# ScalarE scales the whole last h, POOL adds up unit 14, unit 0's k and v products go by batch, and both ends of the order are new

## The reference

```python
h = layernorm(x)
q, k, v, g = h @ Wq.T, h @ Wk.T, h @ Wv.T, h @ Wg.T     # 8 heads of 16
q, k = rope(q), rope(k)
kv = einsum('bshd,bshe->bhde', k, v); ksum = k.sum(1); vsum = v.sum(1)
num = einsum('bshd,bhde->bshe', q, kv) * scale + vsum
den = einsum('bshd,bhd->bsh', q, ksum) * scale + 256
o = num / den + conv5(v)                                # 5 taps along the rows, and a bias
x = x + (o * g) @ Wo.T
h2 = layernorm(x)
y = fp8_round(h2 / s_in) @ fp8_round(K / s_k) * (s_in * s_k)
x = x + bf16(y) + bias
```

## Time and profile before

| | us |
|---|---|
| median of 3 runs | 168.31 (168.03 to 168.59) |
| the profiled execution | 168.34 |
| its span, from the first instruction to the last | 166.5 |
| PE busy | 151.6 (91%) |
| DVE busy | 149.7 (90%) |
| POOL busy | 133.9 (80%) |
| ACT busy | 125.6 (75%) |

### The profile page before, as it was taken

One profiled execution on the slowest core, in us unless ns is written; L12 is line 12 of the kernel. 1 busy time (PEld: TensorE's weight loads), 2 busy tenths in 40 slices (PEclk: granted clock), 3 DMA queues, 4 the chain that ended last, 5 costly groups with the idle time before them and its releaser, 6 DMA issues.

```text
span 166.5 us, 3671 instructions
## 1 busy us (share of the span) xinstructions
PE 151.6 (91%) x1047; PEld 122.7 (74%) x1047; DVE 149.7 (90%) x279; ACT 125.6 (75%) x342; POOL 133.9 (80%) x162
## 2 busy tenths in 40 slices
PE   7599989999999999999999999999999999998530
PEld 2176888896868888888979786898978788875410
DVE  1368999989989999999999999999999999999583
ACT  4769791666997889788898998856698887666931
POOL 1456898784989799989999989968879797998850
PEclk9999999999999999999999999999999999999985
DMA  4931520210151617252736132227122423104113
GB/s 140 274 122 41 128 63 17 52 32 4 33 126 32 195 32 210 76 138 65 216 127 164 56 100 63 65 45 238 35 77 58 96 76 84 31 4 157 65 63 126
DMA packets 16390, 15.51 MB, mean 93 GB/s; under 512 B 8944, under 2 KB 10352, under 8 KB 16368
## 3 DMA queue, kind: packets, MB, share of 16 engines
q1 hardware_dynamic: 15936, 14.99, 32.9%
q10 hardware_dynamic: 432, 0.26, 0.6%
HBM read 5.02 MB, written 4.19 MB: 55 GB/s over the span
## 4 chain that ended last, share of the span: by engine, by line
PE 56%; DVE 17%; issue 11%; ACT 7%; POOL 6%; DMA 2%; DVEq 1%; ACTq 0%; POOLq 0%
PE bank L1276 6%; PE bank L1302 6%; PE p_num L1321 6%; DVE acc L981 6%; PE p_num L1313 6%; PE bank L1266 6%; PE bank L1340 6%; PE bank L1257 5%; PE bank L1284 5%; PE bank L1249 4%; PE bank L1330 3%; PE bank L1292 3%; ACT h L441 2%; POOL rs L661 2%; DMA xs<-in_x_dram 2%
## 5 line engine op out<-in xcount | busy, mean ns | idle before, releaser
L981 DVE SCALAR_TENSOR_TENSOR acc<-bank,columns,acc 128x510 f32<-128x510 f32 (+1 forms) x48 | 34.7, 723 | 0.3 <-ACT outer L413 0.3
L441 ACT ACTIVATE h<-x,nmr,rs 128x128 bf16<-128x128 f32 x60 | 24.7, 483 | 3.8 <-POOL nmr L664 3.3
L383 ACT ACTIVATE h<-xs,nmr,rs 128x128 f32<-128x128 f32 x64 | 26.2, 484 | 0.5 <-POOL nmr L653 0.5
L661 POOL TENSOR_TENSOR rs<-ve,minus_half 128x4 f32<-128x4 f32 (+1 forms) x17 | 16.6, 977 | 10.0 <-ACT ve L432 10.0
L697 POOL TENSOR_TENSOR k<-k_turned 128x512 f32<-128x512 f32 x16 | 20.4, 1274 | 4.5 <-DVE k_turned L966 4.5
L706 POOL TENSOR_TENSOR acc<-acc,outer 128x508 f32<-128x508 f32 x16 | 20.3, 1267 | 2.3 <-DVE acc L981 2.3
L650 POOL TENSOR_TENSOR rs<-ve,minus_half 128x4 f32<-128x4 f32 (+1 forms) x17 | 16.6, 976 | 5.7 <-ACT ve L374 5.6
L966 DVE TENSOR_TENSOR k_turned<-bank,turn_k 128x1024 f32<-128x1024 f32 x16 | 19.5, 1220 | 1.2 <-PE bank L1266 0.9
L690 POOL TENSOR_TENSOR qT<-q_turned,q_swapped 128x512 f32<-128x512 f32 x16 | 20.4, 1274 | 0.1
L954 DVE TENSOR_TENSOR q_turned<-bank,turn_q 128x1024 f32<-128x1024 f32 x16 | 19.5, 1217 | 0.9 <-PE bank L1257 0.7
L1302 PEld LDWEIGHTS bank<-v,k 128*128 128x128 f32 x128 | 16.6, 190 | 4.5 <-issue 3.1
(11 more groups left out here) (81 smaller groups left out, 334.7 us busy)
## 6 DMA issues: line engine op xcount, KB each, us to landing
q_swapped<-q_turned SPq DMA_DIRECT2D x32, 128.0 KB, 2.3
xs<-in_x_dram SPq DMA_DIRECT2D x15, 256.0 KB, 3.3
out_dram<-ob SPq DMA_DIRECT2D x15, 256.0 KB, 2.5
xs<-in_x_dram SPq DMA_DIRECT2D x2, 128.0 KB, 2.9
turn_q<-in_turn_q_dram SPq DMA_DIRECT2D x1, 256.0 KB, 4.5
out_dram<-ob SPq DMA_DIRECT2D x2, 128.0 KB, 2.0
h2T<-h SPq DMA_TRANSPOSE x14, 2.4
w_qk<-in_w_qk_dram ACTq DMA_DIRECT2D x1, 128.0 KB, 2.9
```

The lines of the kernel that those rows point to most:

```text
L383: last = nc.scalar.activation(h[:, s, t], xs[:, u % NX, t], ACT.Identity, scale=rs1[:, s, t:t + 1], bias=nmr1[:, s, t:t + 1])
L441: last = nc.scalar.activation(h2[:, s3, t], x2[:, u % 4, t], ACT.Identity, scale=rs2[:, s, t:t + 1], bias=nmr2[:, s, t:t + 1])
L981: nc.vector.scalar_tensor_tensor(out=part, in0=p_vT[:, :, lo + off:hi + off], scalar=conv_w[:, k:k + 1], in1=part, op0=ALU.mult, op1=ALU.a ...
```

## The change

Five things are changed.

- **The last half's h2.** end_norm2 goes to ACT for both batches; DVE's is gone.
- **Unit 14's sums.** add_bias(14) and final_sum(14) go back to POOL, with the semaphores of every other unit.
- **Unit 0's products of k and v** are split by batch (j=0, j=1), and k is now first, ahead of q, and v last.
- **The orders** of all five queues are new for units 0 to 4 and from unit 10 or so to the end; the loops in the middle keep their order within a unit (ACT keeps one turn of its loop and writes out units 7 to 9 with small exchanges).
- **PSUM banks** of unit 0's first transposes, unit 14's transposed h2 and unit 15's halves are others, and the semaphores named in PE's list go with them.

```diff
-        p_h2T = bank[5][:, 0:W // 2].bitcast(BF16)
+        p_h2T = bank[4][:, 0:W // 2].bitcast(BF16)
...
-        late_yc_done = sem("late_yc_done")
-        late_ob_done = sem("late_ob_done")
...
-            def end_norm2():
+            def end_norm2(j):
                 s, s3 = LAST % 2, LAST % 3
-                act.wait_ge(nmr2_done, count_last(LAST, j=0))
+                act.wait_ge(nmr2_done, count_last(LAST, j=j))
                 act.wait_ge(h2T_in[s3], h2T_count(LAST - 3))
-                for t in range(TPB):
+                for t in tiles_of(j):
                     last = nc.scalar.activation(h2[:, s3, t], x2[:, LAST % 4, t], ACT.Identity,
                                                 scale=rs2[:, s, t:t + 1], bias=nmr2[:, s, t:t + 1])
-                last.then_inc(end_h2_done[0], 1)
+                last.then_inc(end_h2_done[j], 1)
...
             quantise_if_small(13, is_small)
             norm2(14)
             move_y(13)
+            quantise_if_small(14, is_small)
             var_eps2(15, 0)
-            quantise_if_small(14, is_small)
             var_eps2(15, 1)
-            end_norm2()
             move_y(14)
+            end_norm2(0)
+            end_norm2(1)
             end_quantise(0, is_small)
             end_quantise(1, is_small)
             end_move_y()
...
             add_k(1)
+            round_ffn_weights()
             add_q(1)
             add_k(2)
-            round_ffn_weights()
...
             pow2(14)
             add_bias(12)
             final_sum(12)
+            add_bias(13)
             pow2(15, 0)
             pow2(15, 1)
-            add_bias(13)
+            add_bias(14)
             final_sum(13)
+            final_sum(14)
...
-            end_norm2()
-            add_bias(14)
             end_quantise_if_wide(is_small)
             end_half(0)
-            final_sum(14)
             end_half(1)
...
-            def project_k(u, *freed):
-                pe.wait_ge(hT_done, count_first(u))
+            def project_k(u, *freed, j=None):
+                pe.wait_ge(hT_done, count_first(u, j=j))
...
-                for t in range(TPU):
+                for t in tiles_of(j):
...
-                last.then_inc(k_filled, 1)
+                if j != 0:
+                    last.then_inc(k_filled, 1)
...
-            project_q(0)
-            project_v(0)
+            project_k(0, j=0)
+            project_k(0, j=1)
+            project_q(0, (hT_done, count_first(0, j=1)))
             sum_v(0)
-            transpose_v(0, (hT_done, count_first(0, j=1)))
-            project_k(0, (v_done, count(0)))
+            project_v(0, (k_turned_done, count(0)), j=0)
+            project_v(0, j=1)
             transpose_h(1, (q_turned_done, count(0)))
```

More of the change, by code:

```diff
@@ L491, in _ @@
             var_eps1(1)
+            norm1(1)
+            move_v(0)
             var_eps1(2)
-            move_v(0)
-            norm1(1)
+            move_hT(1)
             conv_middle(0)
-            move_hT(1)
             conv_outer(0)
-            norm1(2)
             var_eps1(3)
             move_v(1)
+            norm1(2)
             move_hT(2)
-            var_eps1(4)
[L503 to L508, removed]
+            conv_outer(1)
+            conv_middle(1)
+            norm1(3)
+            move_v(2)
+            move_hT(3)
+            var_eps1(4)
             var_eps2(0)
@@ L512, in _ @@
             norm2(0)
-            move_hT(4)
+            norm1(4)
             move_v(3)
@@ L527, in _ @@
             norm1(5)
+            var_eps2(2)
             quantise_if_small(1, is_small)
-            var_eps2(2)
             move_hT(5)
             move_y(1)
[L532 to L552, removed]
+            for t in range(6, 7):
                 norm2(t - 4)
@@ L562, in _ @@
                 move_hT(t)
+            norm2(3)
+            move_v(6)
+            var_eps1(7)
+            conv_middle(6)
+            conv_outer(6)
+            quantise_if_small(3, is_small)
+            norm1(7)
+            var_eps2(4)
+            move_hT(7)
+            move_y(3)
+            norm2(4)
+            move_v(7)
+            var_eps1(8)
+            conv_middle(7)
+            conv_outer(7)
+            quantise_if_small(4, is_small)
+            norm1(8)
+            var_eps2(5)
+            move_y(4)
+            move_hT(8)
+            norm2(5)
+            move_v(8)
+            round_identity()
+            var_eps1(9)
+            conv_middle(8)
+            conv_outer(8)
+            quantise_if_small(5, is_small)
+            norm1(9)
+            var_eps2(6)
+            move_y(5)
+            move_hT(9)
+            norm2(6)
+            move_v(9)
+            var_eps1(10)
+            conv_middle(9)
+            conv_outer(9)
+            var_eps1(11)
+            quantise_if_small(6, is_small)
+            norm1(10)
+            var_eps2(7)
+            move_y(6)
+            move_hT(10)
             norm2(7)
-            var_eps1(11)
             move_v(10)
             var_eps1(12)
+            norm1(11)
             conv_middle(10)
-            norm1(11)
-            var_eps1(13)
             conv_outer(10)
             quantise_if_small(7, is_small)
+            var_eps1(13)
             move_hT(11)
@@ L759, in _ @@
             sum_outer(5)
-            for t in range(8, 11):
+            add_k(6)
+            pow2(4)
+            add_q(6)
+            add_bias(3)
+            pow1(8)
+            final_sum(3)
+            sum_outer(6)
+            for t in range(9, 11):
                 add_k(t - 2)
@@ L1083, in _ @@
             gate(1)
+            invert(2)
             conv_tap(2, 2)
[L1085 removed]
+            divide(2)
             dve.wait_ge(w_ready, 1)
@@ L1122, in _ @@
                 conv_tap(t - 1, 2)
+            mask_kv(8)
+            add_lepe(7)
+            stats1(10)
+            gate(7)
             stats1(11)
+            turn_q_unit(9)
+            turn_k_unit(9)
+            quantise_if_wide(6, is_small)
+            residual(7)
+            conv_tap(9, 0)
+            stats2(7)
+            invert(8)
+            conv_tap(9, 1)
+            divide(8)
+            conv_tap(9, 2)
             mask_kv(9)
```

361 lines of the change are left out of this document (170 added, 191 removed).

## The result

The changed kernel takes 165.60 us (median of 6 runs, 165.41 to 165.86), the kernel before on the same chip 168.16 (168.03 to 168.59): ratio 0.9845, 95% interval 0.983 to 0.986, so 2.6 us faster. The forecast was 166.9, 1.3 too slow.

A forecast was written before the change was run, and what follows sets the result against it. TensorE and VectorE, both all but full, were taken to bound the middle, leaving start and end to win: 168.34 - 1.2 (start) - 0.24 (end) = 166.9 us, range 165.5 to 168.2.

The forecast's parts named there:

- Unit 0: Start: k first, in halves; first tap at 14.85 against 14.93, VectorE's set of work ending 0.36 us ahead.
- The holes: VectorE's waits ahead of residual(1), 0.78 us, and mask_kv(4), 0.47 us, get filled or closed.
- The lead: Time won at the start and carried through the full middle: 1.2 us, from bounds of 0.36 and 1.5.
- POOL at the start: Rounding done at 24.6, following POOL work at 33.5, hidden ahead of attend(2) by only 0.25 us.
- rival (c): POOL late ahead of attend(2) at the start; at 2.5 us late the time is 169.2; chance 0.08.
- less 0.2: End: slightly earlier unit 14 statistics give back 0.2 us, leaving the second batch's project_o(15) 0.68 late.
- ScalarE's scaling: End: ScalarE's last two scalings take 0.9 us after the last nmr, ending at 159.8 instead of 160.72.
- VectorE's wait for POOL: End: the last half's bias waits for POOL's sum, priced between nothing and 1.15 us, taken in full; end gains 0.24.
- rival (a): End: VectorE's adds don't wait for POOL, so the end gains 1.3 us: 165.8; chance 0.20.
- Landing: End: the last store's time behind the last sum, taken as unchanged, with SyncE's moves costed at nothing.
- (b): Middle, 95 to 143 us: a late piece ahead of TensorE loses the time won at the start: 167.9; chance 0.18.
- (d): End: ffn(13) waits for h2T(13)'s transfer; 1.5 us later puts the end 1.4 later, 168.3; chance 0.06.

The follow-up runs named there:

- the hole run: The changed kernel with VectorE's invert(2) again behind unit 2's last tap and divide(2) behind residual(1): 166.72 us, 1.1 slower.
- the run with the rounding back: The changed kernel with POOL's rounding of the FFN weights moved behind add_q(1) and add_k(2): 168.56 us, 3.0 slower.
- the sums back: The changed kernel with VectorE scaling the second batch and adding up unit 14 as before, move_y(14) behind ScalarE's own scaling: 166.22 us.
- POOL's sum held: The changed kernel with unit 14's sums on idle VectorE, VectorE scaling the second batch and POOL's final_sum(13) held behind that: 165.09 us.
- the end alone: The kernel before with the new end only (late queue orders, ScalarE's scaling, POOL's sums of unit 14), old start: 166.73 us.
- ScalarE's scaling alone: The kernel before with ScalarE scaling both batches of the last h, ahead of move_y(14), all else as before: 167.50 us.

## Why the prediction was right in direction and wrong in size

By its own steps, in the order of the sum:

- **Unit 0.** turn_k(0) at 9.13, turn_q(0) at 10.26, first tap at 14.85: measured 9.17, 10.31, 14.80. Right.
- **The holes.** Both closed as said; the hole run gives 1.1 back, more than the 0.78, since a second wait comes with it. The lead of 1.5 at its best was 1.27 at mask_kv(4), and what was carried 1.0 to 1.1 against 1.2. Right within 0.2. Which of the new orders closed the wait ahead of mask_kv(4) wasn't run alone.
- **POOL at the start.** Rounding done at 24.7 and add_q(2) at 33.7, forecast 24.6 and 33.5. That POOL has little to spare here, as rival (c) had it, shows in the run with the rounding back, 3.0 slower; the wait that grew there first was TensorE's for h(4), not the one for attend(2), and 0.67 of it came through the clock.
- **"With 0.2 for the bf16 transposes, less 0.2 since statistics of unit 14 are a little earlier, it starts at 155.5: 0.68 late."** This is the step that failed, in the term "less 0.2". Without the lead of 1.0, project_o(15,1) starts at 155.0 in the change, against 154.82 in before. VectorE's new order has residual(14) ahead of mask_kv(15) and its statistics ahead of invert(15,0), both of which they followed; the residual starts at 148.32 instead of 150.26 and the statistics at 149.28 instead of 151.23: 1.95 earlier, 0.95 beyond the lead, where the step allowed 0.2. The same term went into "it ends at about 157.0", POOL's add_bias(13), from which the prediction counts the two powers and the last nmr: it ended at 155.3, 156.3 without the lead. The last nmr, forecast 0.6 later than before without the lead, came at the same place. With the statistics put back (and a divide further), project_o(15,1) was 1.0 late, add_bias(13) 1.15, and the kernel 1.1 slower. It is a mis-sized term, worth 0.6 us at the nmr: the walk was done for TensorE's queue with ScalarE's times of before, and not for VectorE's queue ahead of it.
- **ScalarE's scaling** ended 0.9 after the last nmr, as said. On the old order it is worth 0.65; on the new one the run with both assignments turned back lost nothing between the nmr and the last sum. Of VectorE's 2.38 in before, 0.97 went with add_bias(13) beside the scalings (1.41 in that run), and in the new order that bias is away from them, whoever scales.
- **VectorE's wait for POOL.** The bound between nothing and 1.15 was taken at the full wait; measured 1.05 against 0.28, and 0.29 without POOL's sums. Right, and rival (a), which had the measured time almost exactly (165.8), had it for the wrong reason. From the nmr to that bias's end the forecast was 3.45, measured 3.46. Behind it VectorE has three instructions (sum, bias, sum) and took 1.13; the prediction put four and the last, 1.38, and that is all of the difference between 4.83 and 4.59: 0.24.
- **Landing.** The prediction took the stretch behind the last sum as fixed; it shrank by 0.4. That unit 14's store leaves SP's queue 2.8 earlier was in the diff and was not costed: SyncE's moves were put at nothing. With unit 14's sum back inside the last half on VectorE the 0.4 was lost again.

The 1.15 between forecast and the profiled time are thus 0.6 + 0.24 + 0.4 less some 0.1 of lead. Rivals (b), (c) and (d) did not occur. The new PSUM banks, SyncE's moves and add_bias(13)'s new place were not run alone, so what each is worth is read from traces or open.

## What to carry to other kernels

When an instruction moves behind another in one queue, walk the queue that feeds that other in its new order too, before calling the move a loss; a transfer's or transpose's new place can be there to fill a wait. Give the idle engine at the tail the work that stands in the other's way, and look at the store queue as a part of the tail. A loss that appears tens of microseconds behind an edit deserves a look at the DMA rows: the edit may only have moved a transfer into the way of a load, and the next edit may undo that. And a loss that is larger than its wait deserves a look at the granted clock behind the wait.

## What the runs showed of the hardware

- An instruction load of 0.02 MB (q8) that fell among the last packets of a DMA transpose delayed its landing from 2.4 to 4.0 us after the issue (three kernels); one of 0.01 MB (q14) at the same distance went with 3.1 to 3.6, for which there is no controlled pair. At 70 us the changed kernel escapes this by 0.1 to 0.2 us.
- VectorE's bf16 add of 128x256 took 1.05 beside POOL's f32 sum and 0.28 alone, and POOL's sum was held in turn: 1.66 for one, 1.53 in another run, where it takes 1.16. The Trainium skill (SBUF — State Buffer, Who interferes with whom) calls the shared ports an exclusive lock, held for the whole instruction by whichever engine issues first; these rows agree, with VectorE and POOL each on the losing side once.
- The last store's landing went with what was issued before it: 2.1 us with 0.6 between the issues, 2.3 to 2.4 with a 256 KB store within 0.5 ahead of the pair (before, the sums back, POOL's sum held). Whether the order of the stores is the cause was not tested by itself.
- TensorE's granted clock fell from full speed to half of it (2.4 to 1.2 GHz) near the start in two of three traces with the old start: 0.50 from 9 to 12 us in the end alone and in ScalarE's scaling alone, 1.00 in before. q's first product took 1.92 and 2.07 us instead of 1.12. TensorE's last two waits ahead of that product were as long where the clock fell (0.69 and 0.56 in ScalarE's scaling alone) as where it didn't (0.64 and 0.56 in before), so these rows don't tell why it fell. In the run with the rounding back the fall came behind a wait of 2.30.
